# Attention on one core: each key tile's value products split into two column halves, one behind each run of scores

## The reference, cut to what matters

```python
scores = einsum('bhqd,bhkd->bhqk', Q, K) / sqrt(16)   # layer 0 adds -0.1 * |q - k|
attn   = softmax(scores, axis=-1)
out    = einsum('bhqk,bhkd->bhqd', attn, V)
```

## Time and profile before

| | us |
|---|---|
| median of three runs | 954.75 |
| profiled execution | 954.32 |
| its span, first to last instruction | 952.5 |
| TensorE busy | 837.4 (88%) |
| VectorE busy | 573.8 (60%) |
| ScalarE busy | 437.6 (46%) |
| GpSimd busy | 269.0 (28%) |
| exponentials (line 819), 512 of them | 192.6 + 102.8 |
| maxima (line 1110), 256 of them | 300.7 |
| value products (line 537), 1024 records | 138.3 |

### The profile page before, as it was taken

One profiled execution on the slowest core, in us unless ns is written; L12 is line 12 of the kernel. 1 busy time (PEld: TensorE's weight loads), 2 busy tenths in 40 slices (PEclk: granted clock), 3 DMA queues, 4 the chain that ended last, 5 costly groups with the idle time before them and its releaser, 6 DMA issues. The chain is left out here.

```text
span 952.5 us, 11843 instructions
## 1 busy us (share of the span) xinstructions
PE 837.4 (88%) x4356; PEld 500.3 (53%) x4356; DVE 573.8 (60%) x914; ACT 437.6 (46%) x821; POOL 269.0 (28%) x293
## 2 busy tenths in 40 slices
PE   5678999999989889953999999982999999999994
PEld 3334434344336669821444343322678778778764
DVE  4346798989607936725898999919814235135026
ACT  2112787878865376420588877874120210210110
POOL 5522455454432377400000000104311121120221
PEclk9879799999999999985699999995899999998998
DMA  9865222222013300055135322120000000000000
GB/s 283 140 204 141 73 78 72 79 74 69 3 65 113 89 1 1 1 151 161 34 104 164 114 70 72 29 63 2 1 1 1 1 23 1 1 23 1 0 23 23
DMA packets 40538, 60.67 MB, mean 64 GB/s; under 512 B 7256, under 2 KB 17240, under 8 KB 40480
## 3 DMA queue, kind: packets, MB, share of 16 engines
q1 hardware_dynamic: 39616, 58.99, 21.6%
q0 software_dynamic: 864, 0.92, 0.9%
HBM read 40.02 MB, written 18.87 MB: 62 GB/s over the span
## 5 line engine op out<-in xcount | busy, mean ns | idle before, releaser
L1110 DVE TENSOR_REDUCE row_max<-ps_wide 128x2 f32<-128x1024 f32 x256 | 300.7, 1220 | 35.5 <-PE ps_wide L469 35.4
L819 ACT ACTIVATE probs<-ps_a 128x512 f32<-128x512 f32 x342 | 192.6, 604 | 51.4 <-PE ps_a L525 43.8
L469 PE MATMUL ps_wide<-stack_k,stack_q 48*128 48x512 f32 x512 | 160.3, 485 | 36.1 <-DVE planes L1088 22.0
L525 PE MATMUL ps_a<-stack_q,stack_k 62*128 62x512 f32 (+1 forms) x342 | 141.0, 460 | 5.0 <-ACT probs L819 5.0
L537 PE MATMUL ps_out<-probs,vals 128*32 128x512 f32 x1024 | 138.3, 614 | 3.0 <-POOL probs L968 0.5
L915 ACT ACTIVATE hid_full<-ps_a 128x512 f32<-128x512 f32 x32 | 19.1, 598 | 219.4 <-PE ps_a L737 157.7
L819 ACT ACTIVATE probs<-ps_misc 128x512 f32<-128x512 f32 x170 | 102.8, 604 | 21.7 <-PE ps_misc L525 19.8
L525 PEld LDWEIGHTS ps_a<-stack_q,stack_k 62*128 62x128 f32 (+1 forms) x342 | 61.6, 192 | 94.0 <-ACT probs L819 64.8
L968 POOL TENSOR_TENSOR probs<-probs,fixes_sb 128x512 f32<-128x512 f32 x64 | 81.8, 1279 | 88.3 <-ACT probs L819 88.3
L469 PEld LDWEIGHTS ps_wide<-stack_k,stack_q 48*128 48x128 f32 x512 | 68.6, 198 | 71.9 <-DVE planes L1088 22.8
L1029 POOL TENSOR_TENSOR hid_lo<-hid_full,hid_hi 128x512 fp32r<-128x512 f32 x32 | 42.6, 1332 | 196.1 <-ACT hid_hi L916 196.1
(11 more groups left out here) (157 smaller groups left out, 1244.2 us busy)
## 6 DMA issues: line engine op xcount, KB each, us to landing
planes_k<-planes SPq DMA_DIRECT2D x32, 256.0 KB, 3.7
planes_q<-planes SPq DMA_DIRECT2D x32, 256.0 KB, 4.0
stack_q<-planes_q SPq DMA_DIRECT2D x64, 128.0 KB, 2.8
stack_k<-planes_k SPq DMA_DIRECT2D x64, 128.0 KB, 2.8
stack_q<-planes_q SPq DMA_DIRECT2D x64, 64.0 KB, 2.7
stack_k<-planes_k SPq DMA_DIRECT2D x64, 64.0 KB, 2.5
w_e_raw<-in_L_W SPq DMA_DIRECT2D x4, 1024.0 KB, 5.5
ctxT<-in_ctxT SPq DMA_DIRECT2D x4, 512.0 KB, 7.6
```

The costliest lines, as they stand in the source:

```text
L469: mm(raw_slot(("pair", g, p))[:, i * S:(i + 1) * S], stack_q[at, slot(g, c) + q * P:slot(g, c) + (q + 1) * P], stack_k[at, slot(g, c):slot ...
L525: mm(score_slot(("tile", n))[:], stack_k[at, slot(g, c) + k * P:slot(g, c) + (k + 1) * P], stack_q[at, slot(g, c):slot(g, c) + S], start=T ...
L819: do(probs[n % PROBS][:, j, :], score_slot(("tile", n * HG + j))[:], ACT.Exp, scale=0.25).then_inc(exp_done, 1)
L1110: v.tensor_reduce(row_max[:, g % 2, :, p], raw_slot(("pair", g, p))[:].rearrange("p (i k) -> p i k", i=2), AX, ALU.max).then_inc(sem(f"max ...
```

## The change

`weigh` gets a second argument, the part. Each part multiplies 256 of the 512 query columns for all four heads. Part 0 takes the waits and stands behind the first run of scores, raw, raw, scores; part 1 stands behind the second run, and it alone signals `pv_done`. The first product of a group clears the accumulation flags of the bank in part 0 only. At the end of the attention, both parts of the last two k tiles follow each other. The other engines' programs are as before.

```diff
+HALF_S = S // 2
...
-                def weigh(n):
+                def weigh(n, part):
...
-                    pe.wait_ge(probs_ready, n + 1 if l == 0 else HG * (n + 1))
-                    if k == 0:
-                        wait(pe, sem(f"out_kept{l}"), g)
+                    if part == 0:
+                        pe.wait_ge(probs_ready, n + 1 if l == 0 else HG * (n + 1))
+                        if k == 0:
+                            wait(pe, sem(f"out_kept{l}"), g)
+                    cols = slice(part * HALF_S, (part + 1) * HALF_S)
                     for j in range(HG):
-                        mm(po[32 * j:32 * j + VW, :], vals[:, k, g * HG + j, :], probs[n % PROBS][:, j, :],
-                           start=(k == 0), stop=(k == QT - 1)).then_inc(sem(f"pv_done{l}"), 1)
+                        ins = mm(po[32 * j:32 * j + VW, cols], vals[:, k, g * HG + j, :], probs[n % PROBS][:, j, cols],
+                                 start=(k == 0 and part == 0), stop=(k == QT - 1), skip_group_check=True)
+                        if part == 1:
+                            ins.then_inc(sem(f"pv_done{l}"), 1)
...
                             scores(g, k, c, 1)
-                        weigh(g * QT + k - BEHIND)
+                            weigh(g * QT + k - BEHIND, c)
...
                 for n in range(G * QT - BEHIND, G * QT):
-                    weigh(n)
+                    for part in range(2):
+                        weigh(n, part)
```

## The result

The changed kernel takes 973.07 us (median of four runs, 969.87 to 975.74), beside 955.17 for the kernel before (four runs; 954.75 was the median of the first three). The ratio is 1.019, with a 95% interval of 1.015 to 1.024. The changed kernel's profiled execution took 975.74 us, 21.4 more than that of before. Measured again later, its ratio was 1.0175 (1.0131 to 1.0218).

The account below looks back on a forecast made before the run. Bound: the circle of score, exponential, fourth score and products, 2.60 us a k tile. Per layer 47 x 0.14 = 6.6 won, 15 x 0.80 = 12.0 lost; 10.8 over both layers, 954.32 to 965.1, forecast 965, range 951 to 985.

Parts of the forecast that it names:

- the forecast's own 958 to 973: Range of the forecast case itself, chance 0.60, for x (how much cheaper an extra visit is) from 0.06 to -0.06.
- The wait: K tile 2, groups 1 to 15: part 0 waits at line 535 for ScalarE's po copy; 0.80 us lost, 15 times a layer.
- the split's own terms: Plain k tiles: each half 0.34 + 0.32 + 0.57 = 1.23 us, a k tile 2.46, 0.14 less, 47 times a layer.
- the dear visit: Rival, chance 0.18: the 0.42 us from score to products holds before each half; k tile 2.66, time 987.
- The circle of first score, its exponential, fourth score and products: K tile before the change: 0.54 + 0.65 + 0.42 + 0.99 = 2.60 us, said to set the pace.
- The exponentials, VectorE and the correction on GpSimd: At 2.46 us a k tile none is late; VectorE takes a raw pair in 1.22 of 1.23, the correction has over 1 left.
- The cheap exit: Rival, chance 0.12: part 0 signals nothing, so leaving it for the next score is 0.11 us cheaper; time some 952.
- half the signals go: Value products after the split: half of their signals disappear, covering nothing, priced at nothing.
- the free visit: Rival, chance 0.06: TensorE switches between scores and products at no cost, x 0.33; plain k tile 2.28 us, time about 938.
- The clock: Rival, chance 0.04: TensorE standing 1.10 us once a group drops the clock; 30 k tiles lose 1.5 each, time about 1010.

Follow-up runs that it names:

- The early copy: Changed kernel, split kept, with ScalarE's copy out of po moved ahead of k tile 2's first exponential: 941.98 us, ratio 0.985; again 940.42, 0.986.
- the early copy alone: Kernel before, products whole, with ScalarE's copy out of po moved ahead of k tile 2's first exponential: 950.46 us, ratio 0.997.

## Why the prediction was right, step by step

The forecast was 965 in a range of 951 to 985, slower; 973 is the range's upper half and beyond the forecast's own 958 to 973 by a hair. The wait and the split's own terms are right for the reasons given. That the number stayed in the range is in part luck: the upper end was there for the dear visit, which did not come, and what filled it was the clock in layer 1, which the sum had at nothing.

- The circle of first score, its exponential, fourth score and products set the pace: right. Without it TensorE's own list does, at 2.48 a k tile, where I had 2.46. All three terms hold: 0.34, 0.33 (I took 0.32 and feared 0.42) and 0.57.
- The wait at line 535: right in place and count, and nearly in size. It was forecast as 15 x 0.80 a layer. K tile 2 is some 0.82 longer in 25 groups and 0.57 in the four without raws; one more ran at 1.2 GHz. The early copy gives it back.
- The exponentials, VectorE and the correction on GpSimd stay hidden: right, with VectorE nearly full in plain k tiles, its maxima 1.24 apart (4.96 for four).
- The cheap exit: wrong, and seen directly. Part 0 signals nothing and part 1 signals four times, and both are 0.57 from their start to the next score. The Trainium skill's estimate for four increments ("TensorE: Matmul & The Clock Gate", section "The cost: per-tile semaphore tail"), read as the prediction reads it, as a delay of TensorE's own next score, would have set them 0.105 apart; this trace does not agree. The prediction's "half the signals go" is a slip: a k tile still has four, all from part 1, and it was priced at nothing.
- The dear visit and the free visit: both out, by the 0.33 and the 0.57.
- The clock: the mechanism I gave 0.04 came, in another place than I looked. I argued from steady stretches that standing 1.10 us would not make the clock fall, and for the most part it didn't: it is 1.00 between 125 and 275 us. Only in the last group of layer 1 did it fall, at 659 us, and not in the second profile of the same kernel. I did not ask what the change does where the clock is low to begin with. Layer 0's start showed such a place, and I used it for a price alone.

What made 21 of the forecast 11 can be read from the two profiled executions, group by group. Layer 1's start at 1.2 GHz took 13.5 more than the forecast had for its groups 0 to 2. In the other groups with raws, plain k tiles won some 0.13 instead of 0.14 and the wait cost 0.82, not 0.80: 2.4 more, of which 1 is in layer 1's groups 7 to 13, where k tile 1 won nothing. What was missed on the other side: the last two groups of a layer make no raws, so their k tile falls on to 2.18 (264.01 to 266.19 below), and the first of the two took 0.7 less than before in each layer, where I had 0.4 more: 2.2 less. The last group of each layer took 0.1 less and 0.9 more, the latter with the clock's fall at 659 us, together as forecast. In layer 0 the clock rose a k tile earlier than in the profile of before, 1.6 less, and outside the attentions 1.5 went. 10.8 + 13.5 + 2.4 - 2.2 - 1.6 - 1.5 = 21.4, as measured. So the term that was mis-sized is the clock's, which the sum had at nothing: it is 13 us in this profile and 6 in the second one (29.2 against 23.3).

A k tile without raws in the changed kernel:

```profile
264.01 0.49 PE L526 MATMUL ps_a<-stack_q,stack_k 62*128 62x512 f32 x2
264.44 0.64 PE L540 MATMUL ps_out<-probs,vals 128*32 128x256 f32 x8
...
266.19 0.50 PE L526 MATMUL ps_a<-stack_q,stack_k 62*128 62x512 f32 x1
```

## What to carry to other kernels

When work is moved forward in an in-order list, move its waits in your mind first: a wait that cost 0.16 us at the end of a step cost 0.82 more in the middle, with everything that is now queued behind it. Then look at the engine that it waits for, since an idle gap there may take the awaited work earlier, and one line moved on ScalarE turned 1.9% slower into 1.4% faster (2% with layer 1's first two groups left whole). Price the clock at the places where it is low already, not only where it might fall.

## What was not expected of the hardware

- In layer 1 the clock rose late wherever its first products were split. In the five profiles with groups 0 and 1 split, it rose 15 to 36 us behind the start of the first k tile with products, and 3 to 8 such k tiles took over 4 us; in the seven others 4 to 6 us behind it, and one at most did. One of the seven is the run with whole products in k tile 2 alone: there the first k tile with products was whole and the next were split. TensorE was busy for 10.00 of 10 us from 465 to 475 both before and after, so its busy time doesn't show the difference.
- Layer 0 did not behave so: in each profile its clock rose 4 to 10 us behind the start of its first k tile with products, split or not. What sets the two layers apart was not found, and stays open.
- At the end of layer 1, where there are no raws, the clock fell within the attention in three of the twelve profiles: with the split in the changed kernel's first one and in the first with groups 0 and 1 unsplit, and without it in that of the early copy alone. In this last one the two groups without raws took 31.7 us, 7 more than in layer 0, and its single runs lie from 947.77 to 956.89; whether the fall sets that spread was not tested, since one run alone has a profile. The engine table, first of the changed kernel, then of the early copy without the split:

```profile
650.00:659.00 9.00, 7.74 (x74) 3.23 (x66) 1.50 (x4) 7.55 (x15) 0.00 (x0) 1.00 0.26 77
659.00:664.00 5.00, 5.00 (x52) 1.90 (x50) 0.00 (x0) 2.26 (x5) 0.00 (x0) 0.66 0.00 0
```

```profile
600.00:618.00 18.00, 16.51 (x102) 6.17 (x103) 13.15 (x22) 14.81 (x31) 3.30 (x8) 1.00 0.01 2
618.00:636.00 18.00, 16.77 (x62) 4.78 (x55) 1.50 (x4) 9.61 (x19) 0.00 (x0) 0.56 0.32 82
```
